# First attention of a two-layer transformer block: 16 single score slots become 8 double ones, and routing follows two batches behind

## The reference

```
q, k, v = heads(norm(x) @ Wq.T + bq), heads(ctx @ Wk.T + bk), heads(ctx @ Wv.T + bv)
scores  = q @ k.T / sqrt(8)  -  1e9 where mask_q != mask_k
x       = x + softmax(scores) @ v                # per batch and head, 256 x 256
logits  = norm(x) @ W_router + b_router          # top 2 of 8 experts per token
x       = x + sum over the 2 experts: w_e * (relu(norm(x) @ W1[e] + b1[e]) @ W2[e] + b2[e])
```

## Time and profile before

| | |
|---|---|
| three runs | 831.14, 838.76, 841.51 us; median 838.76 |
| the profiled execution | 843.45 us, span of the trace 841.5 us |
| mean granted clock of TensorE | 0.884 of 2.4 GHz |
| busy in the span | PE 694.4, DVE 480.5, ACT 395.8, POOL 374.7 us |
| first attention and routing | about 21 to 260 us of the span |

### The profile page before, as it was taken

One profiled execution on the slowest core, in us unless ns is written; L12 is line 12 of the kernel. 1 busy time (PEld: TensorE's weight loads), 2 busy tenths in 40 slices (PEclk: granted clock), 3 DMA queues, 4 the chain that ended last, 5 costly groups with the idle time before them and its releaser, 6 DMA issues.

```text
span 841.5 us, 16921 instructions
## 1 busy us (share of the span) xinstructions
PE 694.4 (83%) x5142; PEld 525.2 (62%) x5142; DVE 480.5 (57%) x1326; ACT 395.8 (47%) x1115; POOL 374.7 (45%) x579
## 2 busy tenths in 40 slices
PE   2998888988870899948999999899999786399990
PEld 1666665655540788837667767676767554299980
DVE  6756667667414455533765676666665662366664
ACT  2145555545431566625675565656565540133320
POOL 6411465442343355540444555555545463245551
PEclk9999788778555899978999999999999996599995
DMA  9000000000003121231000000000101100212215
GB/s 300 20 13 8 32 26 27 26 26 14 15 13 114 46 56 54 63 118 55 27 21 19 8 27 7 27 11 21 35 21 32 29 12 13 61 46 57 58 46 150
DMA packets 38523, 36.86 MB, mean 44 GB/s; under 512 B 5742, under 2 KB 34676, under 8 KB 38166
## 3 DMA queue, kind: packets, MB, share of 16 engines
q1 hardware_dynamic: 28230, 19.10, 8.0%
q0 software_dynamic: 5616, 12.11, 4.4%
q10 hardware_dynamic: 4592, 4.59, 1.9%
HBM read 25.11 MB, written 11.58 MB: 44 GB/s over the span
## 4 chain that ended last, share of the span: by engine, by line
PE 46%; issue 14%; POOL 13%; DVE 13%; ACT 6%; DMA 5%; SPq 3%; POOLq 0%; DVEq 0%; ACTq 0%
PE ps L601 7%; PE ps L622 5%; PE ps L433 5%; PE ps L464 5%; POOL work L1634 4%; PE ps L406 4%; POOL dispatch L1569 3%; PE ps L612 3%; DVE work L1077 3%; DVE mx L1353 2%; POOL work L1633 2%; ACT work L946 2%; PE ps L638 2%; DMA work<-dispatch 2%; PE ps L684 1%
## 5 line engine op out<-in xcount | busy, mean ns | idle before, releaser
L1077 DVE TENSOR_REDUCE work<-ps 128x2 f32<-128x512 f32 x128 | 86.8, 687 | 68.4 <-PE ps L438 60.2
L946 ACT ACTIVATE work<-ps,nb 128x128 f32<-128x128 f32 (+1 forms) x256 | 104.3, 420 | 42.5 <-DVE nb L1360 38.1
L1617 POOL DMA_INDIRECT results<-work,dsti x78 | 76.6, 982 | 91.8 <-DVE work L1318 31.2
L827 ACT ACTIVATE work<-ps 128x512 f32<-128x512 f32 x128 | 74.5, 599 | 81.1 <-PE ps L433 77.6
L1633 POOL TENSOR_TENSOR work<-work,rc 128x256 f32<-128x256 f32 x64 | 39.4, 615 | 152.9 <-DVE rc L1368 152.8
L601 PE MATMUL ps<-w_up,chib 128*128 x351 | 87.6, 378 | 1.9
L1353 DVE TENSOR_REDUCE mx<-ps 128x6 f32<-128x768 f32 x64 | 61.1, 954 | 39.4 <-PE ps L671 38.9
L1569 POOL DMA_INDIRECT dispatch<-pay,sloti x64 | 65.6, 1026 | 34.4 <-DVE sloti L1149 18.1
L622 PE MATMUL ps<-w_dn,work 128*128 x546 | 74.1, 276 | 1.9 <-DVE work L1321 0.9
L638 PE MATMUL ps<-hl,ra 128*128 128x256 f32 x384 | 63.3, 306 | 7.6 <-ACT work L922 4.5
L433 PE MATMUL ps<-ra 32*128 32x256 f32 x256 | 62.5, 394 | 8.1 <-DVE work L1077 5.4
(11 more groups left out here) (162 smaller groups left out, 1444.6 us busy)
## 6 DMA issues: line engine op xcount, KB each, us to landing
work<-dispatch SPq DMA_DIRECT2D x78, 64.5 KB, 1.8
stage<-in_wgu ACTq DMA_DIRECT2D x16, 176.0 KB
ct<-in_ctxT SPq DMA_DIRECT2D x16, 128.0 KB, 2.6
w_dn<-in_w SPq DMA_DIRECT2D x1, 2048.0 KB, 9.9
stage<-in_w POOLq DMA_DIRECT2D x8, 256.0 KB, 3.1
ybuf<-results SPq DMA_DIRECT2D x16, 128.0 KB, 2.5
work<-results SPq DMA_DIRECT2D x8, 256.0 KB, 5.0
stage<-in_w1p POOLq DMA_DIRECT2D x3, 512.0 KB, 4.3
```

Of the source, the lines that this page charges most:

```text
L946: ac = act.activation(p1[:, pp % 2, e, cols], bk[:, cols], ACT.Exp, scale=SC1, bias=nb1[:, pp % 2, e, t:t + 1], accum_out=rs1[:, pp % 2, e ...
L1077: ve.tensor_reduce(mx0[:, g // 2, :, 32 * j + 26 + g], ps[:, n % 2, :].rearrange("p (t n) -> p t n", t=QT), AX, ALU.max).then_inc(s["a_max ...
L1617: po.indirect_dma_start(yc[l], bass.IndirectOffsetOnAxis(ap=dsti[:, k:k + 1], axis=0), ye[:, k, :], None, bounds_check=TOPK * T - 1, oob_i ...
```

## The change

The loop over 16 heads becomes one over `R0 = 8` double slots. Slot r makes k q.T of heads 2r and 2r+1 (banks 2 and 3) and q k.T of the two heads h ^ 2 (exclusive or) of the next batch (banks 0 and 1): for r = 0 the heads 0, 1 and 2, 3, so all four row groups. One instruction of VectorE takes the maxima over both banks, one of ScalarE the exponentials. A slot now waits for the readers of the slot before it. `pt0` grows from 8 to 20 heads, `low_base` gets two buffers, and the order within a step is written anew: all four mixes of a batch come one step after its scores, untransposing at the end of that step, and adding to x, statistics, logits, choice, slot numbers and sends two steps after the scores. Steps run from -1 to 6, and `last0` handles batch 7 and the routing of batches 5, 6 and 7. The mixes of each batch stay 64 matmuls, the score products 64.

```diff
+PT = 5 * HB
+R0 = H // 2
...
-for k in range(-1, B + 1):
+for k in range(-1, B - 1):
...
 def scores0
+        if r % 4 == 0:
+            pe.wait_ge(*after(0, "qk_ready", 4 * no(c) + 2 + r // 2))
+        need(pe, s["a_max"], R0 * no(c) + r)
...
+            for e, h in enumerate(heads):
+                g, j = divmod(h, HB)
+                rows = slice(32 * j, 32 * j + 32)
+                mk = pe.matmul(ps[:, 2 + e, t * S:(t + 1) * S], kb[rows, par(b), g, t * P:(t + 1) * P],
+                               qb[rows, par(b), g, :], start=True, stop=True)
...
+            for e, h in enumerate(heads):
+                g, j = divmod(h ^ 2, HB)
+                rows = slice(32 * j, 32 * j + 32)
+                mq = pe.matmul(ps[:, e, t * S:(t + 1) * S], qb[rows, par(c), g, t * P:(t + 1) * P],
+                               kb[rows, par(c), g, :], start=True, stop=True)
...
 TensorE, body0
+    c, c2, d, d2 = off(b, 1), off(b, 2), off(b, -1), off(b, -2)
+    has2, here, behind, behind2 = ahead(b, 2), ahead(b, 0), ahead(b, -1), ahead(b, -2)
+    scores0(b, c, 0)
+    project0(c, 2)
+    if here:
+        need(pe, s["o_mul"], no(b) - 1)
+        transpose_max(b, 1)
+    scores0(b, c, 1)
+    if behind:
+        mix0(d, 0)
+    if has2:
+        transpose_x(0, c2, (s["qm_ready"], 2 * no(b) + 2) if here else None)
+    scores0(b, c, 2)
+    project0(c, 3)
+    if behind:
+        mix0(d, 1)
+    scores0(b, c, 3)
+    if behind:
+        mix0(d, 2)
+    if behind2:
+        transpose_t2(0, d2, after(0, "x_split", no(c2) + 1) if has2 else (s["qm_ready"], 2 * no(b) + 2))
+    scores0(b, c, 4)
+    if has2:
+        project0(c2, 0)
+    if behind2:
+        pe.wait_ge(*after(0, "t2_evac", no(d2) + 1))
+    transpose_max(c, 0)
+    scores0(b, c, 5)
+    if behind2:
+        logits(0, d2, (s["qm_ready"], 2 * no(c) + 1))
+    if behind:
+        mix0(d, 3)
+    scores0(b, c, 6)
+    if has2:
+        project0(c2, 1)
+    if behind2:
+        prefix(0, d2, after(0, "idx_done", 2 * no(d2) + 2))
+    scores0(b, c, 7)
+    if behind:
+        pe.wait_ge(*(after(0, "hp_done", no(d2) + 1) if behind2 else (s["qm_ready"], 2 * no(c) + 1)))
+        untranspose0(d)
+    values0(c, after(0, "qk_ready", 4 * no(c) + (5 if has2 else 4)))
+def last0(b):
+    c, d, d2 = off(b, 1), off(b, -1), off(b, -2)
+    scores0(b, c, 0)
+    pe.wait_ge(s["o_mul"], no(d2) + 1)
+    transpose_max(b, 1)
+    mix0(d, 0)
+    scores0(b, c, 1)
+    mix0(d, 1)
+    scores0(b, c, 2)
+    transpose_t2(0, d2, (s["qm_ready"], 2 * no(b) + 2))
+    mix0(d, 2)
+    scores0(b, c, 3)
+    logits(0, d2, None)
+    mix0(d, 3)
+    scores0(b, c, 4)
+    prefix(0, d2, after(0, "idx_done", 2 * no(d2) + 2))
+    scores0(b, c, 5)
+    pe.wait_ge(*after(0, "hp_done", no(d2) + 1))
+    untranspose0(d)
+    scores0(b, c, 6)
+    mix0(b, 0)
+    mix0(b, 1)
+    scores0(b, c, 7)
+    mix0(b, 2)
+    mix0(b, 3)
+    transpose_t2(0, d, (s["o_mul"], no(d) + 1))
+    logits(0, d, None)
+    untranspose0(b, 0)
+    prefix(0, d, after(0, "idx_done", 2 * no(d) + 2))
+    transpose_t2(0, b, after(0, "hp_done", no(d) + 1))
+    logits(0, b, None)
+    prefix(0, b, after(0, "idx_done", 2 * no(b) + 2))
...
 ScalarE
+def exps0(b, r):
+    act.wait_ge(s["b_psum"], R0 * no(b) + r + 1)
+    if r % 2 == 0:
+        need(act, *after(0, "pv_psum", 4 * no(b) + r // 2 - 4))
+    h = (H * no(b) + 2 * r) % PT
+    act.activation(pt0[:, h:h + 2, :], ps[:, 2:4, :], ACT.Exp, scale=SC0).then_inc(s["b_exp"], 1)
...
 VectorE
+def row_max(c, r):
+    g, j = divmod(2 * r ^ 2, HB)
+    ve.wait_ge(s["a_psum"], R0 * no(c) + r + 1)
+    if r % 4 == 0:
+        need(ve, s["mt_psum"], 2 * no(c) - 1 + r // 4)
+    k = 32 * j + 26 + g
+    ve.tensor_reduce(mx0[:, g // 2, :, k:k + 33:32].rearrange("p t e -> p e t"),
+                     ps[:, 0:2, :].rearrange("p e (t n) -> p e t n", t=QT), AX, ALU.max).then_inc(s["a_max"], 1)
...
 VectorE, body0
+    for r in range(R0):
+        row_max(c, r)
+        if not here and r in (2, 3, 4, 5, 6, 7):
+            rest_of_ln0(r - 2)
+        if r == 0:
+            if here:
+                place_max(b, 1)
+            if behind2:
+                added0(d2)
+        if r == 1:
+            if behind2:
+                stats(0, d2, 1)
+            if has2:
+                x_low(0, c2)
+        if r == 2:
+            qk0(c, 2)
+        if r == 3:
+            qk0(c, 3)
+        if r == 4:
             place_max(c, 0)
+        if r == 5 and behind2:
+            choose(0, d2)
+        if r == 6:
+            if has2:
+                qk0(c2, 0)
+            if behind2:
+                place(0, d2)
+        if r == 7:
+            if has2:
+                qk0(c2, 1)
+            if behind:
+                attend0(d, (0, 1))
+def last0(b):
+    d, d2 = off(b, -1), off(b, -2)
+    added0(d2)
+    stats(0, d2, 1)
+    place_max(b, 1)
+    choose(0, d2)
+    place(0, d2)
+    attend0(d, (0, 1))
+    added0(d)
+    stats(0, d, 1)
+    choose(0, d)
+    attend0(b, (0, 1))
+    added0(b)
+    stats(0, b, 1)
+    place(0, d)
+    choose(0, b)
+    place(0, b)
...
 POOL, body0
+    d2, c2, c3 = off(b, -2), off(b, 2), off(b, 3)
+    if ahead(b, 2) and no(b) >= 0:
+        po.wait_ge(*after(0, "qk_psum", 4 * no(c2) - 4))
+        context_split(0, c2)
+    if ahead(b, -2):
+        leave0(d2)
+    if ahead(b, 3):
+        if no(c3) == 2:
+            roots0(2, 4, TT)
+        norm_in0(c3)
     q = no(b) + 1
...
+    split_piece(piece0, F0, q, q + 1 < E)
+    if ahead(b, -2):
+        place0(d2)
+def last0(b):
+    d, d2 = off(b, -1), off(b, -2)
+    leave0(d2)
+    place0(d2)
+    leave0(d)
+    place0(d)
+    for w in range(2):
+        po.dma_start(stage[:, w, :], a["w1p"][:, w * 1024:(w + 1) * 1024]).then_inc(s[f"st_in{w}"], 16)
+        had[w] += 1
+    leave0(b)
+    place0(b)
 
```

More of the change, by code:

```diff
@@ L571, in _ @@
             batches(body0)
+            last0((0, B - 1))
             def experts(l):
@@ L1199, in split_bias, with added0 @@
                                         op1=ALU.add).then_inc(s["bias_ready"], 1)
+            def added0(b):
+                attend0(b, (2,))
+                ve.wait_ge(*after(0, "x_add", no(b) + 1))
             def body0(b):
[L1203 to L1240 removed]
@@ new lines, in last0 @@
+            def last0(b):
[15 more added lines that the diff above has]
+                place(0, b)
+                weight_gap(0)
+                table(0)
+                weigh(0)
@@ L1577, in send, with leave0, place0 @@
                         send_one(l, b, t, ch)
-            def body0(b):
-                if ahead(b, -1):
-                    inverse_root(0, off(b, -1), 1)
-                    norm_out0(off(b, -1))
-                    pack(0, off(b, -1))
+            def leave0(b):
+                inverse_root(0, b, 1)
+                norm_out0(b)
+                pack(0, b)
+            def place0(b):
+                count_seen(0, b)
+                send(0, b)
+            def body0(b):
+                d2, c2, c3 = off(b, -2), off(b, 2), off(b, 3)
[8 more added lines that the diff above has]
+                    norm_in0(c3)
                 q = no(b) + 1
@@ L1587, in body0, with last0 @@
                     load(0, piece0, F0)
-                if q < E:
-                    split_piece(piece0, F0, q, q + 1 < E)
-                if ahead(b, 3):
-                    c = off(b, 3)
-                    po.wait_ge(*after(0, "qk_psum", 4 * no(c) - 4))
-                    context_split(0, c)
-                    if no(c) == 2:
-                        roots0(2, 4, TT)
-                    norm_in0(c)
-                if ahead(b, -1):
-                    count_seen(0, off(b, -1))
-                    send(0, off(b, -1))
-                if no(b) == B - 1:
-                    for w in range(2):
-                        po.dma_start(stage[:, w, :], a["w1p"][:, w * 1024:(w + 1) * 1024]).then_inc(s[f"st_in{w}"], 16)
-                        had[w] += 1
+                split_piece(piece0, F0, q, q + 1 < E)
+                if ahead(b, -2):
+                    place0(d2)
+            def last0(b):
+                d, d2 = off(b, -1), off(b, -2)
+                leave0(d2)
[7 more added lines that the diff above has]
+                place0(b)
             po.wait_ge(s["slots_blank0"], 16)
             batches(body0)
+            last0((0, B - 1))
             po.wait_ge(s["wl_split"], 1)
```

213 lines of the change are left out of this document (71 added, 142 removed).

## The result

The changed kernel took **809.46 us** (median of 4 runs, 806.81 to 812.14) beside 837.96 for the kernel before (4 runs, 831.14 to 841.51): a ratio of 0.967 (0.960 to 0.974), faster by 3.3%. The forecast was 818 with a range of 800 to 842. The sum had -20.6 us; the medians are 28.5 apart. The profiled execution took 807.82. The only trace of the kernel before is from one of its slower executions (843.45 us), so the two traces differ by 35.6 us, 7 more than the medians, and differences read from the two traces may be too large by that much.

The account below looks back on a forecast made before the run. It took TensorE as nearest to its bound before, and the VectorE-TensorE loop (full clock) or TensorE (half clock) after. Terms 0 - 5.2 - 19.4 + 4 = -20.6 us took 838.76 to 818 us; range 800 to 842.

Parts of the forecast that it names:

- better clock: Rival, chance 0.22: less half clock than 43%; with 20% a step is 20.6 us, -34 in all, 804 us.
- Scores, row groups: Score products on TensorE: 16 slots become 8 double ones, each 0.45 us at full clock and 0.73 at half.
- TensorE at half clock, 27.9 a step: TensorE's work per step summed to 27.9 us at half clock, bound by TensorE; about 15 us at full clock.
- VectorE and the loop, 19.3 a step at full clock: Full-clock step bound by the VectorE-TensorE loop at 19.3 us, with single-buffered slots and maxima of 1.22 us.
- Steps 1 to 6, -19.4: Six middle steps at an unchanged 43% half clock: 22.2 us each, 133.5 together, a gain of 19.4 us.
- Step 0, -5.2: Step 0, at half clock, with three mixes moved to step 1: 22.2 us in place of 27.4.
- Step -1, 0: First step, bound by VectorE: maxima fall from 11.0 to 9.8 us, two uncovered handovers give that back; no change.
- POOL's move, 0: POOL's context split, normalising and sends moved within the steps: its 13 us fit in 19.3, costing nothing.
- The tail, +4: Two batches of routing left to last0: +8.0 us, against -4 for a denser TensorE; +4, between -1 and +8.
- Everything after: The kernel after 260 us: no change in length expected; any change would show the prediction wrong.
- A reader's wait: Rival, chance 0.18: each of eight maxima a step still waits 1.12 us for scores; step 24.6 us, total 836 us.
- Half clock throughout: Rival, chance 0.15: slot gaps keep the clock at 1.2 GHz from step 1 on; step 29.0 us, total 862 us.

Follow-up runs that it names:

- the repeat: The changed kernel measured once more, with no edit, on the chip of three follow-up kernels: 803.89 us, 0.967 of the kernel before.
- fillers: The changed kernel with 89 idle matmuls on TensorE where its profile shows half clock: 800.04 us, 0.961 of the kernel before.
- the third set: Four kernels on one chip: the kernel before with idle matmuls (846.79 us) and three combinations of edits on the changed kernel (795.17, 807.65, 795.27 us).

## Why the prediction was right, point by point

The total of 809.46 lies in the range of 800 to 842 and just inside the forecast's own 808 to 830, but one of the signs that the prediction named against itself came: the half-clock share was 18%, outside 30 to 55%. That the total is inside all the same is owed to the width of the range, which took in the rival with the better clock. By the medians the gain is 28.5 us, between the forecast's 20.6 and that rival's 34. The terms, from the two traces:

- **Scores, row groups.** Right: 0.44 us at full clock. The 0.59 us that the 3.07x of the Trainium skill (TensorE: Matmul & The Clock Gate, Measured speedup vs the span model) would give, an estimate, isn't there. The Trainium skill's page TensorEngine Tiling (Array Packing), section Theoretical Speedup, has up to 4x for a dimension of 32; no run here uses one row group alone, and from two to four of them eight products go from 0.66 to 0.44 us. Without the row groups a full-clock step is 1.2 us longer (19.8 against 18.6) and step 0 3.2.
- **TensorE at half clock, 27.9 a step.** None of steps 1 to 6 ran at half clock throughout, so this term stays unmeasured by itself. Its counterpart at full clock, "about 15 us", is too small: TensorE was busy 16.2 us a step in the repeat (64.87 in four).
- **VectorE and the loop, 19.3 a step at full clock.** Measured 18.6 with no disturbance, 18.6 to 19.6 in the first profile. The maximum is 1.224 us as computed, the handover 0.14. My model made the loop the bound of nearly every slot; it is that of four in eight, and a step is therefore less sensitive to the maxima than the sum would have it: 4.3 us less of them brought 1.8, two short ones in place of a long one cost 0.2. So the merged instruction is not the saving; whether the saving is the one handover where there were two, or the waits that the new order moved away, no run separates.
- **Steps 1 to 6, -19.4.** The mis-sized term: measured -32.1 from trace to trace. The step that failed is "all matmuls stay the same in number, so I take the same share of half clock, 43%". It was 18%. With 0.18 the same formula, 1 / (0.82/19.3 + 0.18/27.9), gives 20.4 a step and 122.5 for six, against 120.7 measured: by that formula 11 of the missing 12.7 us are the clock share. In the repeat 0.99, 1.00 and 0.77 over 17.8, 74.2 and 20.1 us make 9%, and six steps are 112.1.
- **Step 0, -5.2.** Measured -5.3, but the clock rose for 3.4 us inside it (0.87 in the view, and half-clock sizes before it at 1.00), so part of the agreement is luck. The kernels with batch 7 normalised first and with the sends moved ran all of it at half clock, as the prediction had it: 22.5 and 22.4, beside the forecast's 22.2, and 4.2 to 4.3 us under the 26.7 of the same marks before. At full clock for most of it, with fillers, it is 18.5.
- **Step -1, 0.** Measured +2.4. TensorE's waits for VectorE there grew from 3.4 to 7.0 us: 5.0 of them for the subtractions of the projections (L1158), which stand ahead of single-buffered double slots and cost 1.6 with the second buffer. "Two uncovered handovers" was too few.
- **POOL's move, 0.** Right in the steps: POOL is busy 12.1 us of an 18.6 us step in the repeat, and TensorE doesn't wait for it. The reason given, "the spare 6 us", is not the one that counts (its 13 us of work are not in the rows either, which give 11.2). The packed rows are ready 0.9 to 1.1 us before TensorE turns them, and with the sends moved back TensorE waited 1.6 us for them in three steps.
- **The tail, +4.** Measured +2.2 (+0.8 in the repeat). The term of POOL's queue is confirmed by its removal: of its 8.0 us placing, sends and loads are 6.5, for which the timeline has 7.3, and the tail is 29.8 without them, 7.4 to 8.8 shorter. The clock was 0.72 instead of 0.50, and it stands against that term as the -4 did. The row read for "223.5 to 248", 24.2 us busy of 36.5, is that of 223.5 to 260; up to 248 TensorE was busy 20.3 of 24.5 us, so the tail before was denser than the sum took it.
- **Everything after.** 581.6 before, 579.0 after, 584.7 in the repeat: no effect beyond its own scatter, as forecast.

Of the rivals, *a better clock* (0.22) came out in its size: it has 20% at half clock, 20.6 a step and -29, and 18%, 20.1 and -32 were found. Its total of 804 is 5.5 below the median of 809.46, the forecast's 818 is 8.5 above it. *A reader's wait* fell: the maxima waited 17.0 us in 18 waits in place of 42.6 in 38, and 5.8 us over four undisturbed steps. *Half clock throughout* fell at step 1.

Where the clock comes from is shown in part. It is not the amount of matmul work in a step, which is the same. What the traces tie it to are gaps of TensorE. In the twelve traces with double slots every one of the 18 falls inside steps 1 to 6 comes within 4 us of the start of a gap of 1.0 us or more; ten such gaps had no fall behind them. Where the gap was filled, the fall was gone (step 6 with idle matmuls). In steps 2 to 5 of the repeat, all at full clock, no gap is over 0.53 us. The kernel before has two gaps of TensorE in each step that it runs at full clock: 0.82 us ahead of a mix, which waits for `attend0`, and 0.92 ahead of `prefix`, which comes right behind the choice of experts. Four of its eight falls (93.3, 117.2, 141.1, 195.7) come in the second of these or within 0.3 us of its end; this is the row behind the one of 117.2:

```profile
117.78 0.17 PE L506 MATMUL ps<-seen,cbi 128*128 128x16 bf16 x1 [0.92 <-issue]
```

The new order does both a step later, and these gaps aren't there. That this is what keeps its clock is argued and not shown: the kernel before fell behind shorter gaps than the changed kernel did, and no run changes the place of `prefix` alone. The share of time that TensorE is busy doesn't decide it: the kernel with two row groups and split readers held full clock for 106 us in a row with 54 us of 60 busy, the repeat for 102 with 65 of 74. And the double slots hold the clock only where nothing disturbs them; with late readers, in the third set, they lost it again and again. The argument set against the *better clock* failed: it took the busy stretches at half clock for the cause of the half clock.

So, over six steps from the only trace of the kernel before to the repeat (152.8 to 112.1): at full clock 23.1 at most to 20.0 for the order, 20.0 to 18.6 for row groups and readers, 4.5 a step or 27 us at most. What remains, some 14 us, is half clock that no longer occurs, but this split is loose: the trace of the kernel before is from an execution of 843.45 us, and on the chip of the repeat that kernel took 832.81, 10.6 less.

## What to carry to other kernels

Before merging two readers for the sake of the longer instruction, look at the order around them: the new order, with one semaphore round trip for two tiles and routing a batch later, was worth up to 3 us of a 23 us step, the merged instructions 0.2. When a step runs now at full clock and now at half, list the gaps of the matrix engine ahead of each fall before filling it with idle work; here they were waits of 1 us and more. When work moves one batch later, look at the in-order queue of the slowest issuer in the epilogue; here putting one normalisation ahead of four sends is worth another 1%. And don't carry a share of half clock from one order to another: price both levels, and put the share of each case into the range.

## What the runs showed of the hardware

- Eight 32-row float32 products of 256 columns in four row groups take 0.45 us at full clock, four in two row groups 0.43, and eight in two row groups 0.66 (1.15 at half clock against 0.73).
- The clock fell behind short gaps of TensorE: 2.25, 1.88 and 1.08 us in steps 1 to 6 of the changed kernel, 1.04 to 2.7 in its variants, and in the kernel before four times of eight 0.92. After a fall TensorE was busy 3.40 of 3.40 us and 6.50 of 6.80, and then the clock rose again. Full clock held through four steps with 83 to 95% busy.
- A reduction over 1024 elements of two banks takes 1.224 us, two over 512 back to back 1.29. Two exponentials of 512 back to back take 1.09 against 1.024 for one of 1024.
- In one set of four kernels, and in the first profile of the changed kernel, readers started 0.7 to 2.3 us after their scores about once a step, in nine other traces not. Four indirect sends hold POOL's queue for about 5 us (1.0 us each, 1.3 to 1.4 apart).
